# Powers and statistics of live norms only, and two scatters a step earlier, in the final stream of a language-model tower

## What is computed

```
h = tower(tokens)                       # 2 layers, ends with layer norm and a projection to 128
u = layernorm(h)                        # plain
x = layernorm(u) * g1 + b1              # then scan, projection, convolution of 5 taps
y = u + retention(x)
y = y + W2 gelu(W1 (layernorm(y) * g2 + b2))
h = h + y
v = layernorm(h)
e = argmax(v Wg + bg);  p = softmax(v Wg + bg)[e]
out = h + p * (relu(v W1[e] + b1[e]) W2[e] + b2[e])
```

## Time and profile before

| | us |
|---|---|
| median of 3 runs | 919.44 |
| lowest, highest | 919.04, 920.62 |
| profiled execution, its own time | 919.02 |
| its span from the first to the last instruction | 916.9 |

### The profile page before, as it was taken

How to read it: one execution, slowest core, us unless ns; L and a number is a source line. 1 busy time by engine, 2 the same in 40 slices (tenths; PEclk the granted TensorE clock), 3 DMA queues, 4 the chain that set the end, 5 groups by cost and what they waited for, 6 DMA issues and landing times.

```text
span 916.9 us, 23665 instructions
## 1 busy us (share of the span) xinstructions
PE 809.2 (88%) x8467; PEld 617.3 (67%) x8467; DVE 634.4 (69%) x1959; ACT 563.3 (61%) x1559; POOL 567.2 (62%) x820
## 2 busy tenths in 40 slices
PE   5979998999999989989999899999998986887397
PEld 2757766576777666667776666677766664876397
DVE  2769975547899655578997553689975436988454
ACT  2858885437788853267888543778885423565164
POOL 3638885545388856475888554438885546759345
PEclk8989998999999999999999999999999996997599
DMA  2310000142000012430000024200000245001331
GB/s 65 105 47 3 4 13 11 58 139 77 6 4 3 13 35 87 114 92 26 3 3 14 11 81 116 79 5 4 3 3 2 79 121 205 1 3 41 93 103 39
DMA packets 38595, 43.84 MB, mean 48 GB/s; under 512 B 7162, under 2 KB 33881, under 8 KB 38345
## 3 DMA queue, kind: packets, MB, share of 16 engines
q1 hardware_dynamic: 18348, 19.40, 7.1%
q10 hardware_dynamic: 17860, 18.19, 6.7%
q0 software_dynamic: 2272, 4.74, 1.7%
HBM read 20.70 MB, written 21.59 MB: 46 GB/s over the span
## 4 chain that ended last, share of the span: by engine, by line
PE 59%; DVE 21%; issue 5%; SPq 4%; POOL 4%; ACT 4%; DMA 3%; POOLq 0%; DVEq 0%; ACTq 0%
PE bank L1369 7%; DVE p L1011 6%; DVE nmx L1002 5%; PE bank L1575 5%; PE bank L1457 5%; PE bank L1576 5%; PE bank L1506 4%; PE bank L1530 4%; PE bank L1395 3%; PE bank L1406 3%; PE bank L1460 2%; PE bank L1509 2%; PE bank L1680 2%; PE bank L1601 2%; PE bank L1689 2%
## 5 line engine op out<-in xcount | busy, mean ns | idle before, releaser
L573 POOL TENSOR_TENSOR p<-p 128x384 f16<-128x384 f32 (+1 forms) x320 | 283.8, 907 | 103.4 <-ACT p L746 98.7
L1002 DVE TENSOR_REDUCE nmx<-bank 128x1 f32<-128x384 f32 (+1 forms) x384 | 190.6, 511 | 20.7 <-PE bank L1460 16.2
L744 ACT ACTIVATE p<-bank 128x384 f32<-128x384 f32 (+1 forms) x384 | 170.9, 452 | 54.3 <-PE bank L1509 38.0
L1506 PE MATMUL bank<-stack 103*128 103x128 bf16 x1056 | 145.1, 222 | 5.6 <-DMA stack<-mtr 5.1
L746 ACT ACTIVATE p<-bank 128x384 f16<-128x384 f32 (+1 forms) x320 | 144.3, 451 | 0.0
L1509 PE MATMUL bank<-bandb,idb 128*128 128x128 bf16 x672 | 135.3, 222 | 0.0
L1530 PE MATMUL bank<-vst,p 128*128 128x49 bf16 x2112 | 115.8, 185 | 15.2 <-DVE p L1011 13.6
L1457 PE MATMUL bank<-stack 100*128 100x384 bf16 (+1 forms) x384 | 121.2, 316 | 7.3 <-DVE nmx L1002 2.9
L1530 PEld LDWEIGHTS bank<-vst,p 128*128 128x128 f16 x2112 | 89.5, 97 | 32.4 <-DVE p L1011 19.1
L1506 PEld LDWEIGHTS bank<-stack 103*128 103x128 bf16 x1056 | 88.3, 98 | 29.7 <-issue 14.5
L1460 PE MATMUL bank<-bandb,idb 128*128 128x128 bf16 x672 | 101.2, 220 | 0.0
(11 more groups left out here) (253 smaller groups left out, 1818.0 us busy)
## 6 DMA issues: line engine op xcount, KB each, us to landing
xs<-zrow ACTq DMA_DIRECT2D x8, 2193.0 KB, 13.5
xt<-xs SPq DMA_DIRECT2D x23, 129.0 KB, 2.1
w2s<-in_w SPq DMA_DIRECT2D x4, 576.0 KB
mwbs<-in_mwb SPq DMA_DIRECT2D x1, 2064.0 KB, 8.5
mw2s<-in_mw SPq DMA_DIRECT2D x1, 2048.0 KB, 12.8
lnrow<-in_lnr SPq DMA_DIRECT2D x4, 480.0 KB
stack<-mtr SPq DMA_DIRECT2D x96, 3.0 KB
w1b<-in_w SPq DMA_DIRECT2D x4, 291.0 KB
```

Of the source, the lines that this page charges most:

```text
L573: nc.gpsimd.tensor_tensor(p2[:, u % RING, 0:w], p32[:, u % RING, 0:w], p1[:, u % RING, 0:w], ALU.subtract).then_inc(p2_pool, 1)
L744: ins = nc.scalar.activation(p32[:, s % RING, 0:w], ps[2 + s % 3][:, 0:w], ACT.Exp)
L1002: nc.vector.tensor_reduce(nmx[:, vn % 3, h:h + 1], nat_bank(v)[:, 0:w], AX.X, ALU.max, negate=True).then_inc(max_done, 1)
L1506: ins = mm(ps[2 + s % 3][:, blk(i)], stack[0:K_ALL, H + h, blk(m)], stack[0:K_ALL, h, blk(n)], start=True, stop=m == n)
```

## The change

A list LAGS gives the distance in steps of the four norms, and `norms(t)` the range of those that have a block in step t: in steps 0 to 2 norm 0; 3 to 6 norms 0 and 1; 7 to 10 norms 0 to 2; 11 to 15 all; 16 to 18 norms 1 to 3; 19 to 22 norms 2 and 3; 23 to 26 norm 3.

- `bn_aggr` and the epsilon are done for that range alone; the folded variance only where norm 1 is in it (steps 3 to 18).
- The folded variance moves to column 0 of `vin` and the others one up, so that the live columns are a contiguous range, and the power covers this range. The indices in the five normalisations follow.
- The three memsets go.
- GpSimd may send two blocks a step from step 24 on, not from 27 on.

```diff
--- before.py
+++ after.py
@@ -75,6 +75,7 @@
 T0 = 320
 U = NB * H
 ORDER = (1, 2, 3, 0, 4, 5, 6, 7)
+LAGS = (0, 3, 7, 11)
 CHOSEN = tuple(e - 1 + DEPTH for _, e in GROUPS)
 ROW = U - LEAD
 
@@ -413,6 +414,11 @@
 
             return ps[6 + v % 2] if v < LEAD else ps[v % 2]
 
+        def norms(t):
+
+            alive = [k for k, lag in enumerate(LAGS) if 0 <= t - lag < NN]
+            return (min(alive), max(alive) + 1) if alive else None
+
         def early_step(j, part):
 
             return -LEAD + PARTS * (j - 3) + part if j >= 3 else None
@@ -633,11 +639,13 @@
                     pool.wait_ge(y_added, i + 1)
                     nc.gpsimd.tensor_tensor(h0[:, i, :], h0[:, i, :], x1[:, i, :], ALU.add).then_inc(xh_ready, 1)
                 if t < NN + DEPTH - 2:
+                    a, e = norms(t)
+                    a, e = (0 if a <= 1 < e else a + 1), e + 1
                     pool.wait_ge(stats_ready, t + 1)
-                    nc.gpsimd.tensor_tensor(rs[:, t % 2, :], vin[:, t % 2, :], colc[:, 3:4].to_broadcast([P, 5]),
+                    nc.gpsimd.tensor_tensor(rs[:, t % 2, a:e], vin[:, t % 2, a:e], colc[:, 3:4].to_broadcast([P, e - a]),
                                             ALU.pow).then_inc(rs_ready, 1)
                 placed = max([0] + [e for (_, e), c in zip(GROUPS, CHOSEN) if t >= c + 2])
-                for _ in range(1 if t < NN + DEPTH - 2 else 2):
+                for _ in range(1 if t < NN + DEPTH - 5 else 2):
                     if sent < placed:
                         scatter(sent)
                         sent += 1
@@ -1094,9 +1102,6 @@
             nc.vector.memset(tiles[:, 3, :], 1.0)
             nc.vector.memset(more[:, :], 0.0)
             nc.vector.tensor_scalar(tof[:, 2, :], tile_no, -float(P), float(P), ALU.mult, ALU.add)
-            nc.vector.memset(vin[:, :, :], 1.0)
-            nc.vector.memset(mean[:, :, :, :], 1.0)
-            nc.vector.memset(sums[:, :, :], 1.0)
             ch.link(nc.vector.tensor_copy(trow[:, :, 2 * DM + 1].bitcast(I32), token))
 
             def choose(q):
@@ -1168,12 +1173,15 @@
                         dve.wait_ge(kept, i + 1)
                         s_link = ch.mark(nc.vector.bn_stats(sums[:, 1, :], h0[:, i, :]))
                     dve.wait_ge(dve_own, s_link)
-                    for k in range(4):
+                    a, e = norms(t)
+                    for k in range(a, e):
                         ins = nc.vector.bn_aggr(mean[:, w, k, :], sums[:, k, :])
                     ch.link(ins)
-                    nc.vector.tensor_scalar(vin[:, w, 0:4], mean[:, w, :, 1], EPS, None, ALU.add)
-                    nc.vector.tensor_scalar(vin[:, w, 4:5], mean[:, w, 1, 1:2], 1.0 + EPS, EPS * EPS, ALU.mult,
-                                            ALU.add).then_inc(stats_ready, 1)
+                    ins = nc.vector.tensor_scalar(vin[:, w, a + 1:e + 1], mean[:, w, a:e, 1], EPS, None, ALU.add)
+                    if a <= 1 < e:
+                        ins = nc.vector.tensor_scalar(vin[:, w, 0:1], mean[:, w, 1, 1:2], 1.0 + EPS, EPS * EPS, ALU.mult,
+                                                      ALU.add)
+                    ins.then_inc(stats_ready, 1)
                 i = t - 5
                 if 0 <= i < NN:
                     b, n = divmod(i, NB)
@@ -1196,23 +1204,23 @@
                 if 0 <= i < NN:
                     if i >= 2:
                         dve.wait_ge(t0_mm, i - 1)
-                    normal(z0[:, i % 2, :], resid[:, i, :], 0, 0).then_inc(z0_ready, 1)
+                    normal(z0[:, i % 2, :], resid[:, i, :], 0, 1).then_inc(z0_ready, 1)
                 i = t - 4
                 if 0 <= i < NN:
                     if i >= 2:
                         dve.wait_ge(t1_mm, i - 1)
-                    normal(z1[:, i % 2, :], h0[:, i, :], 1, 4).then_inc(z1_ready, 1)
+                    normal(z1[:, i % 2, :], h0[:, i, :], 1, 0).then_inc(z1_ready, 1)
                 i = t - 8
                 if 0 <= i < NN:
                     if i >= 2:
                         dve.wait_ge(t2_mm, i - 1)
-                    normal(z2[:, i % 2, :], x1[:, i, :], 2, 2).then_inc(z2_ready, 1)
+                    normal(z2[:, i % 2, :], x1[:, i, :], 2, 3).then_inc(z2_ready, 1)
                 i = t - 12
                 if 0 <= i < NN:
-                    normal(trow[:, i, 0:DM], trow[:, i, DM:2 * DM], 3, 3).then_inc(z3_ready, 1)
+                    normal(trow[:, i, 0:DM], trow[:, i, DM:2 * DM], 3, 4).then_inc(z3_ready, 1)
                 i = t - 4
                 if 0 <= i < NN:
-                    normal(x1[:, i, :], h0[:, i, :], 1, 1).then_inc(x1_ready, 1)
+                    normal(x1[:, i, :], h0[:, i, :], 1, 2).then_inc(x1_ready, 1)
                 if t in CHOSEN:
                     choose(CHOSEN.index(t))
                 if t - 1 in CHOSEN:
```

## The result

| | before | changed |
|---|---|---|
| median, us (19 runs each, same chip) | 918.9 | 912.95 |
| lowest, highest | 914.34, 920.62 | 906.62, 919.17 |
| mean, standard deviation | 918.37, 1.7 | 913.06, 3.85 |

The ratio is 0.9942 [0.9923, 0.9961], so the change wins 5.3 us (3.6 to 7.1). The forecast was 3.0 us and 916.4; its range ended at 914.7. The direction was right, the size and the range were not.

A forecast was written before the change was run, and what follows sets the result against it. GpSimd's powers and scatters were taken to bound the final stream's tail. Head 0.65, statistics 0.15 and tail 2.2 sum to 3.0 us: 919.02 becomes 916.0, plus 0.42 for the median, 916.4 (chance 0.62); whole range 914.7 to 918.2.

The forecast's parts named there:

- Head: Start of the final stream: the power of step 0, on the chain, gets one column and saves 0.65 us.
- Steps 1 to 22: Final stream: powers off the path save 0; one bn_aggr less at steps 7 and 18 saves 0.15 us together.
- Operand of step 24: VectorE at steps 23 and 24: fewer statistics save 0.28 us a step, so this power's operand comes 0.56 earlier.
- Tail to scatter 10: GpSimd's last powers and scatters: scatter 10 starts 2.2 us earlier, 1.7 if group 2's slots come no earlier.
- Scatter 10 to 15: Last scatters into the expert buffer: spacing unchanged; VectorE's weight copy meets scatter 15 in place of 14, same price.
- Pairing: Two scatters a step from step 24 on: worth 0.4 us of the tail's 2.2.
- late or early clock in the experts: Rivals: TensorE's clock returns late, +1.5, 917.9, chance 0.12; returns early or doesn't fall at 838, 915.1, chance 0.10.
- the choice: Rival: VectorE's late last placing, not GpSimd, sets the tail; group 3's slots hold scatter 14; 918.6, chance 0.06.
- the fixed power: Rival: a power's time is fixed, not by column; only the statistics' 0.15 and 0.56 remain; 918.7, chance 0.07.
- the failed return: Rival: the head's shift makes the clock's return at 777 fail; above 921.3 from three steps on, chance 0.03.
- sum of 3.0: Whole gain in front of the experts: 0.65 head, 0.15 steps 7 and 18, 2.2 tail.
- I allow 1.2 us each way: TensorE's clock beside or behind the edit: its return before the experts may not shift with the work, 1.2 us either way.

The follow-up runs named there:

- e4: Changed kernel with the power of step 0 back at five columns, and the memset this needs: ratio 0.9955 (917.63 us).
- e8: Changed kernel with every power back at five columns, so only statistics and pairing changed, memsets back: 920.35 us in a single run.
- e5: Kernel before, unchanged, run again: 921.71 us in one run, beside 922.84 for one more of the kernel before.
- e14: Kernel before, unchanged, run again: ratio 1.0001.
- e9: Kernel before with 50 unused matmuls in TensorE's idle stretch at the head of the final stream: ratio 1.0012 (920.23 us).
- e12: Kernel before without the GpSimd drain ahead of the last four output scatters: ratio 1.0006.
- e2: Changed kernel with the pairing undone (one scatter a step up to step 26): ratio 0.9928 (913.71 us).
- e3: Kernel before with only the pairing (two scatters a step from step 24 on): ratio 0.9997.
- e1: Changed kernel, unchanged, run again: ratio 0.9938 (916.11 us beside 920.81 for the kernel before).
- e15: Changed kernel, unchanged, run again: ratio 0.9962.
- e13: Changed kernel without the GpSimd drain ahead of the last four output scatters: ratio 0.9947.
- e10: Changed kernel with 50 unused matmuls in TensorE's idle stretch at the head of the final stream: ratio 0.9957 (915.16 us).
- e11: Changed kernel with 50 unused matmuls at the head and 50 more ahead of the wait for the experts: ratio 0.9956 (914.77 us).

## Why the prediction was off

By its steps:

- *Head*, "a 1-column power saves 0.65 us": 0.59 by the first transpose, and by e4 it is worth 0.6 at the head and 0.4 at the experts. The mechanism and the size were right.
- *Steps 1 to 22*, 0.15: 0.31 in the pair. The chain is as described, and the rest is where the clock at the head returned.
- *Operand of step 24*, "0.28 us a step, 0.56 for both": it came 0.78 earlier than the steps before it explain. The statistics gave 0.25 at step 23 and 0.27 at step 24, near the forecast's 0.28 each. The rest, 0.25, is the collision at step 23, which I saw and did not count. Before, GpSimd's sum of block 15 ran from 837.47 to 837.94 beside the normalisation; after, it is over at 836.02, and the normalisation starts at 837.04. The Trainium skill (SBUF — State Buffer, Who interferes with whom) says that the two engines share one pair of ports, under an exclusive lock. The trace agrees here, with 0.60 us beside the sum and 0.35 without it. In e8, where the powers are wide, the sum runs beside the next normalisation instead, which takes 0.48 in place of 0.26.
- *Tail to scatter 10*, 1.64 of the sum: 1.79. Group 2's slots were forecast for 848.6 on the clock of before. That is 847.8 with the 0.8 of the head and of steps 7 and 18; they were ready at 848.14, which is 847.37 when the 0.77 by which this kernel's stream began later is taken off. So they came 0.4 us earlier than forecast, about as much as the two points above gave. (Had they come no earlier at all, the recorded text gets -1.7; its own times give -1.8.) The wait in front of scatter 10 is there, 0.41, of which 0.11 is more than the usual 0.30; I had put that at 0.36.
- *Scatter 10 to 15*, forecast unchanged, "copy then meets scatter 15 in place of 14 at the same price": wrong, 0.36 us were won in the pair, 0.25 against e5 and e14. The scatters are now over at 855.71 and the copy starts at 855.89, so it met none: counted from the feed-forward part the copy came 1.05 earlier and scatter 15 3.83. Nor is the price always the same. In five profiles with the old spacing (the three of the kernel before, e9, e12) the copy starts 0.07 to 0.10 ahead of scatter 14, which takes 1.22 to 1.26. In e2 it starts 0.24 us into scatter 15, and neither is longer than alone (GpSimd's and VectorE's timeline):

```profile
854.09 0.96 POOL L625 DMA_INDIRECT xs<-trow,slot  x1 [0.30 <-issue]
854.33 0.50 DVE L1265 COPY wt<-mwbs 128x644 f32 x1 [1.05 <-issue]
```

- *Pairing*, 0.4 of the tail: 0.6 (e2). It takes the narrow powers to be worth anything (e3).
- *Rivals*: late or early clock in the experts, the choice, the fixed power and the failed return are ruled out in the profiled executions, by the windows, by the single small wait and by the powers' widths.

So in the profiles the sum of 3.0 was too small by 0.7 us in the mean, by 0.9 in the first pair. The term that was mis-sized is the tail: 2.2 forecast, 3.0 in the first pair. A sum of 3.9 would still have left the time in the range. (Added straight, the range's own terms give 914.5 to 918.3 and not 914.8 to 917.9; the measured 912.95 lies outside either.) **The step that failed is "I allow 1.2 us each way" for the clock, with the base of three runs under it.** I looked for the clock's changes in the stretches that the edit touches and took what lies ahead of them as given. It isn't: the last feed-forward matmul ahead of the stream, the same code in all kernels, ended between 750.67 and 758.08 us in the profiles of the study, and the sum of the time at 1.2 GHz ahead of it lay between 23.9 and 47.8 us. Single runs scatter with a standard deviation of 1.7 us for the kernel before and 3.85 for the changed one, and three runs between 919.04 and 920.62 said nothing of that. The interval of the measured difference alone is 1.8 us each way, more than the 1.2 allowed.

That this scatter goes with the clock can be read from the single runs, since each has its mean granted clock on record. In the 19 of the changed kernel it goes from 0.944 to 0.961, and the correlation of time with clock is -0.91. Worked out from clock and span, these runs spent 71 to 103 us at 1.2 GHz, and each microsecond of that goes with 0.33 us of time. In e1 and in the kernel before beside it the correlation is as strong, with 0.37 and 0.23 us.

In numbers, 3.45 us lie between 916.4 and 912.95. The base of three runs was 0.54 above that of 19. The medians differ by 5.95 where the ratio gives 5.3: 0.65. The changed kernel unchanged was timed three times, against the kernel before each time: 5.3, 5.3 (e1) and 3.65 (e15, against e14 and the executions beside both) in the means, 4.6 ± 1.1 pooled over 43 changed executions, so 0.7 are the luck of the first set. (The runs of e1 spent 5.3 us less at 1.2 GHz than those of the kernel before beside them, the runs of e15 2.9 less. At 0.3 us for each that is 0.7 of the 1.65 between their gains.) The last 1.6 is the change being worth 4.6 and not 3.0, and the profiles show 0.7 of it. **Some 0.9 us stay open**, less than the error of 1.1 on the 4.6, so there may be nothing to find. The clock at the head is not shown to be it (in every profile without filler it fell ahead of the first transpose), nor is the drain (e12, e13). One thing stays unexplained beside it: the time at 1.2 GHz ahead of the stream was 34.1 to 47.8 us (mean 41.6) in the 11 profiles of kernels with the changed powers or statistics and 23.9 to 37.5 (mean 30.7) in the 6 of the others, though that code is the same. It makes the changed ones later there, by 2.1 us in the mean, so it doesn't account for the surplus.

No kernel of the study is shown to beat the changed one. Its own three ratios are 0.9942, 0.9938 and 0.9962; e4, e10, e11 and e13 lie among them, and the interval of e2, 0.9928 [0.99, 0.9956], holds two of them.

## What to carry to other kernels

When one engine sets a stretch by itself, price its instructions by their spacing and width; that sum came out within a microsecond. Work out also what the shift separates: two overlaps with another engine went (0.25 and 0.36 us), and I had seen both. And before giving a range for a gain below 1%, look at how the untouched code ahead of the edit varies; if it moves by several us from execution to execution, the range of the median is set by that, not by the edit's sum.

## What the runs showed that I had not expected

- A GpSimd drain is 1.1 to 1.7 us longer (output scatter 18 to 19: 3.32 us against 4.41 to 5.00) in the nine profiles in which a fetch of 16 KB of instructions starts 1.2 to 1.8 us behind the issue of scatter 18, and not in the six others. The two go together in 15 profiles; no experiment moved the fetch alone.
- Filling an idle stretch of TensorE with matmuls moved the fall of the clock from +4.4 to +11.2 us, and not past the sparse steps behind it.
- In the profiles of the experiments the expert loop took 49 to 51 us, in the first two 47.7 and 48.0, in both kernels. In them the interval between tiles 18 and 19 is 3.3 to 3.6 us (4.5 in e9) in place of 1.9. In e1 TensorE waits there 1.12 us for VectorE's weight copy, and VectorE has stood idle for 2.60 us before. The cause is open.
